# Second layer's key blocks turned by VectorE and exchanged through DRAM instead of transposed on TensorE; four PSUM banks for key products instead of two

## What is computed

```python
    def _L1_xattn_ref(hidden_states, cross_attention_states, attention_mask, q_proj_w, k_proj_w, ...):
        NUM_HEADS = 32
        NUM_KV_HEADS = 8
        HEAD_DIM = 128
...
        def rmsnorm(x, w, eps=EPS):
            xf = x.astype(jnp.float32)
            var = jnp.mean(xf * xf, axis=-1, keepdims=True)
```

## Time and profile before

| what | value |
|---|---|
| median of 3 executions | 874.53 us (872.3 to 875.42) |
| the profiled execution | 873.61 us |
| its span, first to last instruction | 871.8 us |
| TensorE busy | 830.1 us (95%), 3984 matmuls |
| VectorE, ScalarE, GpSimd busy | 556.0, 539.0, 550.1 us |
| DMA | 122.74 MB, 73224 packets, mean 141 GB/s |

### The profile page before, as it was taken

How to read it: one execution, slowest core, us unless ns; L and a number is a source line. 1 busy time by engine, 2 the same in 40 slices (tenths; PEclk the granted TensorE clock), 3 DMA queues, 4 the chain that set the end, 5 groups by cost and what they waited for, 6 DMA issues and landing times.

```text
span 871.8 us, 14112 instructions
## 1 busy us (share of the span) xinstructions
PE 830.1 (95%) x3984; PEld 679.2 (78%) x3984; DVE 556.0 (64%) x974; ACT 539.0 (62%) x1785; POOL 550.1 (63%) x557
## 2 busy tenths in 40 slices
PE   6899999999989999999999999999996899999995
PEld 5687888788878888888888888888885667777774
DVE  5505531432566666666666666666666799999996
ACT  4533672134677677767776677776674476767663
POOL 3332452212477777777777777777765368999985
PEclk9999999999999999999999999999999999999998
DMA  8511011003566666666667766667654023333302
GB/s 272 169 49 62 1 49 49 24 25 96 147 187 188 191 186 192 185 181 192 190 181 217 217 189 188 188 187 216 202 155 147 15 106 121 137 144 144 144 1 96
DMA packets 73224, 122.74 MB, mean 141 GB/s; under 512 B 8078, under 2 KB 45838, under 8 KB 73167
## 3 DMA queue, kind: packets, MB, share of 16 engines
q1 hardware_dynamic: 73166, 122.10, 46.4%
HBM read 86.41 MB, written 35.65 MB: 140 GB/s over the span
## 4 chain that ended last, share of the span: by engine, by line
PE 66%; DVE 15%; DMA 7%; ACT 4%; issue 3%; POOL 2%; SPq 2%; DVEq 0%; POOLq 0%; ACTq 0%
PE pair L1381 16%; PE pair L1383 16%; PE pair L1382 16%; PE pair L1537 5%; PE pair L1631 4%; DVE kv L1245 4%; DMA land<-block_bounce 4%; PE pair L1538 4%; DMA block_bounce<-tb 2%; DVE pair L1245 2%; DVE tb L1262 2%; ACT kv L943 2%; SPq L464 1%; ACT prob L872 1%; PE pair L1398 1%
## 5 line engine op out<-in xcount | busy, mean ns | idle before, releaser
L1381 PE MATMUL pair<-split,xnT_hi 128*128 128x512 f32 x288 | 114.2, 397 | 0.3 <-issue 0.3
L1382 PE MATMUL pair<-split,xnT_hi 128*128 128x512 f32 x288 | 112.1, 389 | 0.0
L1383 PE MATMUL pair<-split,xnT_lo 128*128 128x512 f32 x288 | 112.1, 389 | 0.0
L847 ACT ACTIVATE headT<-land 128x512 f32<-128x512 f32 x64 | 40.4, 632 | 100.8 <-DMA land<-block_bounce 87.5
L1381 PE MATMUL pair<-split,aoT_hi 128*128 128x512 f32 x256 | 100.2, 391 | 0.0
L1383 PE MATMUL pair<-split,aoT_lo 128*128 128x512 f32 x256 | 100.1, 391 | 0.0
L1382 PE MATMUL pair<-split,aoT_hi 128*128 128x512 f32 x256 | 100.1, 391 | 0.0
L872 ACT ACTIVATE prob<-pair,nmax 128x128 f32<-128x128 f32 x256 | 89.9, 362 | 13.5 <-DVE nmax L1209 13.3
L1537 PE MATMUL pair<-xnT_hi,split 128*128 128x512 f32 x224 | 89.5, 399 | 6.7 <-DVE tb L1262 3.2
L626 POOL TENSOR_TENSOR prob<-prob,rinv 128x512 f32<-128x512 f32 x64 | 66.6, 1041 | 37.1 <-DVE rinv L1179 37.0
L1538 PE MATMUL pair<-xnT_lo,split 128*128 128x512 f32 x224 | 87.4, 390 | 0.0
(11 more groups left out here) (153 smaller groups left out, 2177.0 us busy)
## 6 DMA issues: line engine op xcount, KB each, us to landing
block_bounce<-tb SPq DMA_DIRECT2D x244, 128.0 KB, 2.3
land<-block_bounce SPq DMA_DIRECT2D x61, 512.0 KB, 3.5
raw<-in_wqo_dram SPq DMA_DIRECT2D x62, 256.0 KB, 3.1
kv<-in_ffn_w_dram SPq DMA_DIRECT2D x14, 768.0 KB, 4.4
kv<-in_ffn_z_dram SPq DMA_DIRECT2D x14, 768.0 KB, 5.6
resid<-in_x_dram SPq DMA_DIRECT2D x2, 1024.0 KB, 8.9
kv<-in_ctx_dram SPq DMA_DIRECT2D x1, 2048.0 KB, 9.4
out_dram<-resid SPq DMA_DIRECT2D x8, 256.0 KB, 2.3
```

The lines of the kernel that those rows point to most:

```text
L1381: pe.matmul(dst, l_hi, r_hi, start=first, stop=False)
L1382: pe.matmul(dst, l_hi, r_lo, start=False, stop=False)
L1383: return pe.matmul(dst, l_lo, r_hi, start=False, stop=last)
```

## The change

1. The four TensorE transposes of each key block and the ScalarE copy behind them are gone. VectorE norms the block in place in PSUM (`key_norm`), then turns its 32x32 squares from PSUM into a half of `tb` (`key_turn`, in the same form as L1195).
2. SyncE writes each turned block to DRAM in four DMAs (`key_write`, 32 partitions x 4 runs of 512 B each) and reads it back in two (`key_read`, 128 partitions x 4 runs of 256 B each), straight to where the scores read it: two key heads lie interleaved there in runs of 32 columns, so the score product's moving operand is 4 runs of 32 columns, 64 apart. Four slots in DRAM, two halves of `tb`.
3. The norm weights `wqk` are applied in the copy to `headT` instead (a `scale` operand of one number per partition).
4. Key products use four banks (6, 7, 4, 5). The attention products of the first layer move from banks 4 and 5 to 0 and 1, this layer norm's transposes from 4 and 5 to 2 and 3.
5. The loads of the value weights move behind the key blocks' DMAs of steps 12 to 15 and behind the last of them. `key_norm` comes ahead of `ln_norm` in VectorE's order. TensorE waits for the last turned block (`s_kt`) ahead of the low-rank products.

```diff
+        key_scr = nc.dram_tensor("key_bounce", (4, KT, 32, KT, P), F32, kind="Internal").ap()
...
+        def key_tile(m, e):
+            pairs = kv[:, 0:2 * QUART].rearrange("p (g t b c) -> p g t b c", g=NKV // 2, t=T, b=KT)
+            return pairs[:, m // T * 2 + e, m % T]
+        def key_columns(pr, e, t):
+            cols = kv[:, bass.ds(pr * 2 * TOK + t * 2 * P, 2 * P)]
+            return cols.rearrange("p (b c) -> p b c", b=KT)[:, :, e * 32:(e + 1) * 32]
...
+            def key_write(m):
+                sp.wait_ge(s_kt, m + 1)
+                if m >= 4:
+                    sp.wait_ge(s_kl[m % 2], 32 * (m // 2 - 1))
+                for quad in range(KT):
+                    sp.dma_start(key_scr[m % 4][:, :, quad, :].rearrange("d e c -> e d c"),
+                                 turned(m)[32 * quad:32 * (quad + 1), :].rearrange("e (d c) -> e d c", d=KT))\
+                        .then_inc(s_kw[m % 2], 16)
+            def key_read(m):
+                sp.wait_ge(s_kw[m % 2], 16 * KT * (m // 2 + 1))
+                for e in range(2):
+                    sp.dma_start(key_tile(m, e), key_scr[m % 4].rearrange("d e b c -> (d e) b c")[:, :, e * 64:(e + 1) * 64])\
+                        .then_inc(s_kl[m % 2], 16)
+            key_write(0)
+            key_write(1)
+            key_read(0)
+            for m in range(3, 2 * T + 2):
+                if m <= 2 * T:
+                    key_write(m - 1)
+                key_read(m - 2)
+                if T + 4 <= m < T + 4 + KT:
+                    weights(WVAL + m - T - 4, WVAL + m - T - 3)
...
             def key_norm(n):
                 dve.wait_ge(s_kr, n + 1)
+                cur = heads(bank[KEY_BANK[n % 4]][:])
+                dve.tensor_tensor(cur, cur, over(rms[:, n % 4, :], P), ALU.mult).then_inc(s_kn, 1)
+            def key_turn(n):
+                dve.wait_ge(s_kn, n + 1)
...
                 if n >= 2:
-                    dve.wait_ge(s_kt, n - 1)
-                dve.tensor_tensor(heads(norm[:, n % 2, :]), heads(bank[6 + n % 2][:]), over(rms[:, n % 2, :], P),
-                                  ALU.mult).then_inc(s_kn, 1)
+                    dve.wait_ge(s_kw[n % 2], 16 * KT * (n // 2))
+                dve.transpose(by_block(turned(n)), split32(bank[KEY_BANK[n % 4]][:])).then_inc(s_kt, 1)
...
-                if m >= 2:
-                    pe.wait_ge(s_kn, m - 1)
+                if m >= len(KEY_BANK):
+                    pe.wait_ge(s_kt, m - len(KEY_BANK) + 1)
...
-                    pe.wait_ge(s_kn, n + 1)
-                    if n >= 2:
-                        pe.wait_ge(s_ke, n - 1)
-                    for h in range(REP):
-                        done = pe.transpose(bank[2 + n % 2][:, tile(h)], norm[:, n % 2, tile(h)], ident[:])
-                    done.then_inc(s_kt, 1)
...
-                    act.activation(by_head(headT[:]), landed(i, 0), ACT.Copy).then_inc(s_qt, 1)
+                    act.activation(by_head(headT[:]), landed(i, 0), ACT.Copy, scale=wqk[:, 0:1]).then_inc(s_qt, 1)
```

More of the change, by code:

```diff
@@ L219, in ln_bank @@
         def ln_bank(k, t):
-            return bank[(4, 5, 0, 1, 4, 5, 7, 0)[t] if k == 3 else 4 + t % 2]
+            return bank[(4, 5, 0, 1, 4, 5, 7, 0)[t] if k == 3 else (2 if k == 1 else 4) + t % 2]
         LN_GROUPS = ((0, HALF), (HALF, HALF + 2), (HALF + 2, T - 1), (T - 1, T))
@@ L226, in split32, with turned, by_block @@
             return ap.rearrange("p (h d e) -> p d h e", h=REP, d=KT)
+        def turned(m):
+            return tb[:, m % 2 * D:(m % 2 + 1) * D]
+        def by_block(ap):
+            return ap.rearrange("p (d h a) -> p d h a", d=KT, h=REP)
         def blocks_of(which):
@@ L430, in _, with weights @@
                 sp.dma_start(dst[:], src).then_inc(s_small, 16)
[L431 to L434, removed]
+            def weights(first, end):
+                for c in range(first, end):
+                    w, c0 = [(w, c0) for w, c0 in ((wq0, WQ0), (wkey, WKEY), (wffn, WFFN), (wval, WVAL))
+                             if c >= c0][-1]
+                    load(c, w[c - c0])
+            for c in range(WQ0, WFFN + KT):
+                weights(c, c + 1)
                 if c == WKEY - 1:
@@ L441, in _ @@
                     sp.dma_start(btb_sb, bTb).then_inc(s_lora, 16)
+            def key_write(m):
[20 more added lines that the diff above has]
+                    weights(WVAL + m - T - 4, WVAL + m - T - 3)
+            weights(WVAL + KT, WGRP)
             for k in range(KT):
@@ L758, in squares @@
                 done.then_inc(s_done, 1)
[L761 to L764, removed]
-                    if m >= 2:
[L766 to L769, removed]
+            for m in range(2 * T):
+                act.wait_ge(s_ka, m + 1)
+                if m >= 2:
+                    act.wait_ge(s_kr, m - 1)
+                if m >= 1:
+                    act.wait_ge(s_ks, m)
+                squares(bank[KEY_BANK[m % 4]], m % 2, s_ks)
                 if 5 <= m < 5 + T:
                     ln_hi(1, m - 5, keep=True)
[L772 to L777, removed]
                 if T + 1 <= m < T + 1 + KT:
@@ L846, in step @@
                         act.wait_ge(s_c, at(p, i))
-                    act.activation(by_head(headT[:]), landed(i, 0), ACT.Copy).then_inc(s_qt, 1)
+                    if i == 0 and p is None:
+                        act.wait_ge(s_wqk, 1)
+                    act.activation(by_head(headT[:]), landed(i, 0), ACT.Copy, scale=wqk[:, 0:1]).then_inc(s_qt, 1)
                 if valid(j + 2):
@@ L1113, in _ @@
                     ln_stats(1, 0)
+                if m >= 3:
+                    key_norm(m - 1)
                 if 3 <= m < 3 + T:
@@ L1116, in _ @@
                 if m >= 3:
-                    key_norm(m - 1)
+                    key_turn(m - 1)
                 if m == 3:
@@ L1444, in keys @@
                     lo_done(pe, WKEY + KT * (kb + 1) - 1)
-                if m >= 2:
-                    pe.wait_ge(s_kn, m - 1)
+                if m >= len(KEY_BANK):
+                    pe.wait_ge(s_kt, m - len(KEY_BANK) + 1)
                 for k in range(KT):
-                    done = three(bank[6 + m % 2][:], ctxT_tile(t, 0, k), ctxT_tile(t, 1, k),
+                    done = three(bank[KEY_BANK[m % 4]][:], ctxT_tile(t, 0, k), ctxT_tile(t, 1, k),
                                  wbuf(kb, 0)[:, k, :], wbuf(kb, 1)[:, k, :], k == 0, k == KT - 1)
@@ L1460, in _ @@
                 pe.wait_ge(s_pe0, b // HALF + 1)
+                if b == 3:
+                    pe.wait_ge(s_pe0, 2)
                 if b >= 4:
@@ L1468, in dense @@
                           wbuf(0, 0)[:, k, :], wbuf(0, 1)[:, k, :], k == 0, False)
[L1470 to L1476, removed]
+            for m in range(2, 2 * T):
+                keys(m)
                 if 4 <= m < 4 + T:
                     ln_transpose(1, m - 4)
[L1479 to L1482, removed]
-                    pe.wait_ge(s_kn, n + 1)
-                    if n >= 2:
-                        pe.wait_ge(s_ke, n - 1)
-                    for h in range(REP):
-                        done = pe.transpose(bank[2 + n % 2][:, tile(h)], norm[:, n % 2, tile(h)], ident[:])
-                    done.then_inc(s_kt, 1)
+            lo_done(pe, WVAL - 1)
+            pe.wait_ge(s_at0, T)
+            for t in range(2):
+                pe.wait_ge(s_xlo, T + t + 1)
+                dense(t)
             pe.wait_ge(s_lora, 32)
+            pe.wait_ge(s_kt, 2 * T)
             pe.wait_ge(s_xlo, 2 * T)
@@ L1625, in step @@
                     n, t = at(p, i), i % T
-                    g = i // T if p is None else 2 * p + i // T
+                    if i == 0 and p is None:
+                        for par in range(2):
+                            pe.wait_ge(s_kl[par], 32 * T)
+                    pr = i // BODY if p is None else p + i // BODY
+                    cols = key_columns(pr, i // T % 2, t)
                     pe.wait_ge(s_qt, n + 1)
@@ L1630, in step @@
                     for h in range(REP):
-                        done = pe.matmul(bank[2 + i % 2][:, tile(h)], headT[:, tile(h)],
-                                         keyT[:, bass.ds(g * TOK + t * P, P)], start=True, stop=True)
+                        done = pe.matmul(bank[2 + i % 2][:, tile(h)], headT[:, tile(h)], cols, start=True, stop=True)
                     done.then_inc(s_c, 1)
```

16 lines of the change are left out of this document (9 added, 7 removed).

## The result

The changed kernel takes 878.0 us (median of 12 runs, 871.2 to 881.3) against 874.4 of the kernel before (12 runs, 872.3 to 875.4): a ratio of 1.0037, with a 95% interval of 1.002 to 1.0053. It is slower by a little, where the prediction had it faster by 3.9 us. The profiled execution took 879.7, with a span of 878.0. It is 6.1 us above the profiled one of before (873.6), while the medians are 3.6 us apart: what follows from the two traces explains the 6.1.

The account below looks back on a forecast made before the run. PE was taken to bound the key stage; 871.8 - 4.0 (PE's earlier low-rank products) + 0.1 (SP) = 867.9 us span, plus 1.8 around it and 0.9 for the median: 870.6 us, range 866.5 to 878.

Parts of the forecast that it names:

- The work removed: Key stage on PE: sixteen transpose groups, 7.0 us, and a 0.9 us bank wait go; low-rank products at 128.6 without new waits.
- The start stall: PE's third layer-norm transpose, at about 95.5 us: PE stands still 3.9 us for DVE's delayed norms.
- Score product: Attention scores: operand in runs of 32 columns priced at nothing for PE, a tenth of 67.4 us kept as bound.
- copy to `headT`: ACT's copy with scale operand: at most 714 for 632 ns in each of 64 steps, hidden by ACT's idle time.
- packets of 256 B: Key reads on the DMA engines: 13.5 to 27 ns each; a block's 1.7 to 2.6 us hidden by SP.
- (c): Rival, 13%: 256 B reads at 60 ns a packet bound the key stage; 882.9 us.
- (d): Rival, 5%: PE pays for strided columns in the score product, a tenth more gives back 6.7 us; 877.3 us.
- The wait of 0.89 us at 88.01: Before `keys(4)` in the old kernel: PE waited for block 3's norm with two banks; four banks remove it.
- SP's block: SyncE's queue: one key block's four writes, two reads and waits take 3.0 us, plus 0.47 with a value weight.
- (b): Rival, 18%: SP lags, 3.5 us per block; turn 15 ends at 135.0, 2.5 later than PE wants it; 873.1 us.
- its margin of 2.0 us: Turn of block 15 ahead of low-rank products: 2.0 us over nine blocks; an SP block may take 3.2 before costing.
- low-rank products, predicted start: PE behind the key stage: 128.6 plus the 3.9 us stall gives 132.5, 4.0 us earlier than before.

## Why the prediction was wrong

**What held.** The work removed is worth what was counted: with every new wait gone the low-rank products start at 128.49 us, for the 128.6 of the prediction. The start stall came where it was put and lasted 3.4 us for 3.9. Score product, copy to `headT` and packets of 256 B cost what they were given (0, hidden, 17.6 ns for 20), so rivals (c) and (d) fall. And the attention loop as a whole takes as long as before, as the first and last start of its 256 products with `aoT_hi` show, before and then changed:

```profile
L1381 PE MATMUL pair<-split,aoT_hi x256: 387/389/628, 245.5 to 686.9; 128*128 128x512 f32 x128
```
```profile
L1435 PE MATMUL pair<-split,aoT_hi x256: 387/389/628, 251.4 to 692.7; 128*128 128x512 f32 x128
```

441.4 us before, 441.3 after; the 5.9 us are lost ahead of the first of them. One reading of the prediction was off, without effect: the wait of 0.89 us at 88.01 is for the norm of block 2, not 3 (bank 6, `s_kn` at 3).

**First wrong term: SP's block.** "3.0 us per block", from rows without reads among the writes, was 3.37: writes 2.0 for 1.76, a read 0.60 for 0.53, and a load 0.62 for 0.47; with one pair of reads at 2.63 the mean is 3.64, loads included. Write 13 was issued 32.7 us behind write 4, where the terms give 27.7: 1.3 us more for the writes, 2.7 for the reads (1.4 of them in the one long pair), 0.3 for the loads and 0.7 for the pauses between. Its landing, from first issue to the start of the turn, took 3.7 us for 3.1. The prediction had written that 3.2 is where it begins to cost. Rival (b) was the right case, to within 0.3 us: it put the end of the last turn at 135.0, and it came at 135.33. That the number fits so well is in part luck: (b) had a surplus of 1.4 us in every third block, and the runs show 0.4 in every block and one of 1.4.

The run with the reads last, which has no lag, and the one with the loads behind, which has 1.6 us less of it, show that this queue is the cause. I gave (b) 18%, and the trace of before had more for it than the row at 281.26: of its groups of four writes from 226 to 296 us, with twice the bytes, five of eleven took 2.03 to 3.19 us, and a read of 512 runs took 0.63 at 209.39.

The long pair is one read, which took 2.06 us at 114.15, and such single long issues stand in the trace of before as well: one write of the group at 281.26 took 1.87. In six of the seven traces with the exchange one issue between 109 and 118 us took 1.0 to 2.1 us. The prediction said that one such costs nothing, which holds only with its margin of 2.0 us. Here write 9 could have gone out 1.1 us earlier without it, as soon as its turn had ended, and TensorE's wait would have been some 0.9 us, an estimate; behind the 0.89 of the earlier trace rows the clock stayed up.

**The step that failed: what a wait costs.** Everywhere the prediction priced a wait at its own length. Case (b) itself was priced at 873.1, which would still have been a little faster. The lower clock behind the waits was left out. For the profiled executions, from PE's timeline:

| | us |
|---|---|
| low-rank products, predicted start | 132.5 |
| start wait, 3.4 for 3.9 | -0.5 |
| half clock behind it: 98.86 to 102.28 is 3.42 us, the same seven steps at full clock 1.83 | +1.6 |
| other, the rest to 133.44 | -0.2 |
| wait for the last turn | +2.0 |
| measured start, 1.1 earlier than before | 135.4 |
| low-rank products at half clock, from their start to the next product, 12.81 - 7.07 | 5.7 |
| 12 dense products at half clock, 5.23 - 2.82 | 2.4 |

So the place behind them is reached 7.0 us later than before (5.7 + 2.4 - 1.1). The same products lie 5.5 us later at 272 us, 6.9 at 800 and 6.1 at 861 (the first by the score products, the others by those of L1537, L1583 in the changed kernel), since the clock falls again in both traces, at different places: at 244 and 859 us before, at 672 and 699 us in the changed kernel. So the span's 6.2 us (878.0 - 871.8) are the 7.0 less what these falls differ by. The position counts as much as the length: the 3.4 us wait had some 3.4 us of lower clock behind it, the 2.0 us wait 17.

The twelve executions of the changed kernel speak for the clock too: ten took 877.0 to 881.3 at a mean granted clock of 0.980 to 0.988, and two 871.2 and 871.8 at 0.996 and 0.992. Those two have no profile, so which of the falls they were spared is not shown.

**A part of it could have been read before.** The trace of the kernel before has such a place, which I did not look at since the change doesn't touch it. Its timeline of PE at 244 us:

```profile
244.41 0.47 PE L1381 MATMUL pair<-probT_hi,vcur_hi 128*128 128x512 f32 x1 [2.25 <-DVE aoT_lo L1184]
244.71 0.54 PE L1382 MATMUL pair<-probT_lo,vcur_hi 128*128 128x512 f32 x1
245.05 0.63 PE L1383 MATMUL pair<-probT_hi,vcur_lo 128*128 128x512 f32 x1
245.47 0.63 PE L1381 MATMUL pair<-split,aoT_hi 128*128 128x512 f32 x1
```

A wait of 2.25 us, and behind it matmuls 0.42 us apart. In the changed kernel the wait of 2.23 at the same place is followed by a spacing of 0.23; this is where the 7.0 us become 5.5. So this fall cost some 1.6 us. With that price the start stall alone moves the forecast from 870.6 to 872, and rival (b) goes from 873.1 to about 876 with both waits, an estimate. The 8 us that the second fall cost could not be read from this row: nothing in the trace of before shows a lower clock that lasts 17 us.

**What stays open.** The runs don't fix what decides whether the clock falls. The ten traces of this case hold the same waits again and again, and the same wait is followed by the lower clock in one and not in another:

| wait of PE | followed by the lower clock in |
|---|---|
| 3.4 us at the start of the key stage | 4 of 4 traces |
| 2.0, 3.2 and 4.0 us ahead of the low-rank products | 3 of 3 |
| 0.4 and 0.8 us at the same place; 0.3 (twice) and 1.5 at the start | 0 of 5 |
| 2.2 to 2.3 us at 235 to 254 us | 6 of 10 |
| 2.9 us at 658 to 675 us | 7 of 10 |
| 0.5 and 1.3 us, close together, at 683 to 702 us | 4 of 10 |
| 2.1 us at 849 to 866 us | 2 of 10 |

So behind a wait of 2 to 3 us the clock may fall or may not, and of the single waits under 1.9 us none was followed by it. The stretch at the lower level was some 3.4 us long nearly everywhere (one was 7, and the last 5 us of the spans are left out); in all three traces in which it began with the low-rank products it lasted 14 to 17 us, to the dense products behind them. Why these small products hold it down is not shown. What makes the one long issue of SyncE isn't either.

## What to carry to other kernels

When a change makes a new wait on a TensorE that is otherwise always busy, look at every wait of that length in the trace of before and read the spacing of the matmuls behind it: the lower clock can cost several times the wait, and it can be absent behind the next wait of the same length. Price a queue's issues from rows with the same neighbours, not from a quieter stretch; where the margin is a few tenths of a microsecond a block over ten blocks, the rival in which it is gone is the forecast. And a wait for the last item of a stage belongs where that item is first needed: moved behind two stages of other work, it was free, and the version with this and two other edits beats the kernel before by 9.1 us.

## What was not expected of the hardware

- A wait of 2.0 us ahead of many short products was followed by 17.5 us at a granted clock of 0.51, with TensorE busy all through it; other stretches at that level were some 3.4 us long.
- Reads of 256 B packets from DRAM took 17.6 ns a packet, less than the 27 ns of 512 B writes.
- Issues of SyncE are not of one length: four writes took 1.75 us alone or behind a pause and 2.0 right behind a read, a load 0.45 and 0.62. One issue in most traces took 1.0 to 2.1 us.
- A second operand for each partition made a copy of ScalarE 92 ns longer (632 to 724). The Trainium skill, "ScalarE: Activation LUTs", What ACT_TABLE_LOAD costs, has about 93 ns for such an operand; the trace agrees.
